# Weight fold from split parts and bias sums off TensorE in an attention and mixture-of-experts kernel

## The chip, the cores and the metric

The kernel runs on one core of one Trainium2 chip. The metric is the device time in microseconds. Its engines are TensorE (PE in the profile, PEld for its weight loads), VectorE (DVE), ScalarE (ACT), GpSimd (POOL), and the queues that issue transfers, SyncE's (SP) above all.

## What is computed

x has two batches of 1024 rows of 512, so 16 tiles of 128 rows. Cut to what matters:

```python
xn = layernorm(x)
q, k, v = split(xn @ w_qkv.T + b_qkv)
s = softmax(q @ k.T / sqrt(512)) @ v @ w_out.T + b_out
h = silu(xn @ expert_w[e] + expert_b[e])       # 8 experts, top 2 per row
m = sum(full_w[e] * h[e]) @ proj_w + proj_b
y = xn + m
g = silu(norm_w * y / sqrt(mean(y * y) + 1e-6))
out = x + s * g
```

All of it is fp32 in and out.

## The kernel before

Products run in fp32r on split operands: a value is written as a high part (a ScalarE copy to fp32r) and a low part (the value less the high part, on VectorE or GpSimd), and `product` makes three matmuls of them, high by high, high by low, low by high. The kernel folds weights first. The value weights times the output weights give `nw`, so that a tile of xn times `nw` is already the projected value (`values`, "v"). The query weights times the key weights give `mw` (`fold_keys`, four of them, in the order FOLDS = 2, 0, 1, 3, "mw").

The order on each engine is written out by hand, with semaphores. The first 71 us go so:

- **SyncE** loads, slice by slice (c = 0 to 3), a slice of the value weights (`raw_v`), one of the output weights (`raw_o`) and two tiles of batch 0 of x (`xb`), then the query and key weights. Then it stores each normalised tile.
- **TensorE** folds the value weights as 16 fp32 matmuls on the raw weights (line 1411; the trace shows two records for each), then makes the value bias with four more (`bias_of_values`), with turns 0 and 1 between and after them. `turn(g)` transposes a normalised tile into `tp` (line 1391). `values(0, t)` are 12 matmuls each (lines 1385 to 1387), with `turn(t + 1)` ahead of tile t. Then come `fold_keys`, `bias_products` (16 matmuls with 1 or 2 stationary columns), turns 8 and 9, the second key fold, `turn_biases`, turns 10 and 11, and the third and fourth key fold, then the logits.
- **VectorE** takes the statistics of the eight tiles of batch 0 (`row_stats`), turns them to mean and inverse deviation in 16 small steps (`first_stats`), normalises tiles 0 and 1, and makes the low parts: `fold_low`, `lo(g)` (x of tile g, "xt_l"), `v_lo` ("v_l"). The statistics of batch 1 lie behind `v_lo` of tiles 3 to 6.
- **ScalarE** makes the high parts (`fold_high`, `hi`, `v_hi`, `qk_high`) and normalises tiles 2 to 15 (line 754).
- **GpSimd** issues the load of x's second batch (line 601), makes the low parts of the query and key weights (`t_l`, `pt_l`, line 607), and then the 23 small steps of `batch_stats` for batch 1 (lines 396 to 406).

A transposed tile or a value product waits for a bank: `turn(g)` for `lo(g - 2)`, `values(0, t)` for `v_lo(t - 2)` and for `lo(t)`.

## Time and profile before

| | us |
|---|---|
| median of 3 runs | 533.2 (532.65 to 533.26) |
| the profiled execution | 533.14 |
| its span | 531.4 |
| TensorE busy | 514.9 |
| VectorE busy | 267.9 |
| ScalarE busy | 201.2 |
| GpSimd busy | 199.7 |

The page is one profiled execution. Line numbers are those of the kernel before. A timeline gives the start and length of each instruction, or of a row of like ones with their count, and in brackets how long the engine had been idle before it and what ended that. A matmul record is longer than the distance to the next, since they are pipelined.

### The profile page before, as it was taken

To read this page: it belongs to the slowest core of one execution; us is meant where nothing else is said; L and a number is where in the kernel's file an instruction comes from. 1 tells how busy PE (TensorE), PEld (TensorE's weight loads), DVE (VectorE), ACT (ScalarE), POOL (GpSimd) and SP (SyncE) were. 2 spreads that over 40 slices of the span, in tenths; PEclk is the share of its full clock that TensorE was granted. 3 is DMA by queue.
4 is the path that set the end of the run, shared out by engine and by line. 5 is a ranking of instruction groups with operands and counts; after the bars stand their busy time and mean duration, and the time that the engine had idled before them with its cause. 6 is when DMAs were issued, how large, how long until landed. Compare 5 with 4: busy or idle time off the path is not lost.

```text
span 531.4 us, 7656 instructions
## 1 busy us (share of the span) xinstructions
PE 514.9 (97%) x2454; PEld 414.7 (78%) x2455; DVE 267.9 (50%) x428; ACT 201.2 (38%) x300; POOL 199.7 (38%) x316
## 2 busy tenths in 40 slices
PE   4999999999999999899999999999999999999995
PEld 2488667887888888788888888888888888888884
DVE  2557232856138255664444444444574854567552
ACT  0265542222034254543333333323363552426550
POOL 3053210000007874243333330435457765266143
PEclk9999999999999799999999999999999999999999
DMA  8761277000100488857755554869523541242202
GB/s 265 270 239 39 93 243 299 0 21 20 41 0 1 178 278 297 283 192 228 245 172 165 165 161 145 301 237 307 169 79 100 198 146 52 83 152 65 79 37 83
DMA packets 37130, 81.40 MB, mean 153 GB/s; under 512 B 4128, under 2 KB 4144, under 8 KB 37104
## 3 DMA queue, kind: packets, MB, share of 16 engines
q1 hardware_dynamic: 27312, 50.60, 26.8%
q0 software_dynamic: 7920, 27.03, 16.6%
q10 hardware_dynamic: 1872, 3.41, 2.2%
q8 instruction: 17, 0.28, 0.2%
q14 instruction: 9, 0.07, 0.0%
HBM read 56.13 MB, written 24.90 MB: 152 GB/s over the span
## 4 chain that ended last, share of the span: by engine, by line
PE 91%; DVE 2%; DMA 2%; issue 1%; POOL 1%; ACT 1%; SPq 0%; ACTq 0%; DVEq 0%
PE ab L1385 19%; PE ab L1387 19%; PE ab L1386 19%; PE tp L1391 9%; PE sc L1385 6%; PE sc L1387 6%; PE sc L1386 6%; PE sc L1411 3%; DMA y_scratch<-yt 1%; DMA raw_o<-in_w_out_t 1%; PE tp L1562 1%; PE sc L1472 1%; PE ab L1419 1%; PE sc L1475 1%; DVE yt L1253 0%
## 5 line engine op out<-in xcount | busy, mean ns | idle before, releaser
L1385 PE MATMUL ab<-W,st_h 128*128 x156 | 64.5, 414 | 1.7 <-DVE st_l L1118 1.7
L1387 PE MATMUL ab<-W,st_l 128*128 x156 | 61.4, 394 | 0.0
L1386 PE MATMUL ab<-W,st_h 128*128 x156 | 60.9, 390 | 0.0
L863 ACT ACTIVATE yt<-yt 128x512 f32<-128x512 f32 x39 | 24.7, 632 | 75.9 <-DVE yt L1253 75.9
L1385 PE MATMUL sc<-xt_h,t_h 128*128 128x512 f32 x128 | 51.5, 403 | 0.0
L1387 PE MATMUL sc<-xt_h,t_l 128*128 128x512 f32 x128 | 50.9, 398 | 0.0
L1386 PE MATMUL sc<-xt_l,t_h 128*128 128x512 f32 x128 | 50.8, 397 | 0.0
L1118 DVE TENSOR_TENSOR st_l<-tp,st_h 128x512 fp32r<-128x512 f32 x40 | 27.7, 691 | 38.9 <-ACT st_h L859 29.2
L664 POOL DMA_INDIRECT y<-y_scratch,pos x32 | 31.0, 970 | 40.8 <-DMA y_scratch<-yt 20.6
L618 POOL TENSOR_TENSOR tile_hot<-in_tile,ids 128x640 fp32r<-128x640 f32 x2 | 6.5, 3242 | 90.0 <-DVE in_tile L1167 90.0
L1253 DVE TENSOR_TENSOR yt<-ab,bias_e 128x512 f32<-128x512 f32 x39 | 27.0, 692 | 26.2 <-PE ab L1387 22.1
L1385 PEld LDWEIGHTS ab<-W,st_h 128*128 128x128 f32 x156 | 29.4, 188 | 7.0 <-issue 2.2
L1184 DVE TENSOR_REDUCE small<-sc 128x1 f32<-128x1024 f32 x16 | 19.6, 1224 | 29.7 <-PE sc L1387 29.6
L1387 PEld LDWEIGHTS ab<-W,st_l 128*128 128x128 f32 x156 | 29.2, 187 | 6.7
L1386 PEld LDWEIGHTS ab<-W,st_h 128*128 128x128 f32 x156 | 29.5, 189 | 5.1
L1008 DVE SCALAR_TENSOR_TENSOR t_l<-ab,tb,t_h 128x512 fp32r<-128x512 f32 x16 | 12.0, 750 | 35.6 <-ACT t_h L773 35.0
L1387 PEld LDWEIGHTS sc<-xt_h,t_l 128*128 128x128 f32 x128 | 24.6, 192 | 5.3
L1386 PEld LDWEIGHTS sc<-xt_l,t_h 128*128 128x128 f32 x128 | 24.8, 193 | 5.0
L1385 PEld LDWEIGHTS sc<-xt_h,t_h 128*128 128x128 f32 x128 | 24.8, 193 | 5.0
L773 ACT ACTIVATE t_h<-ab,tb 128x512 fp32r<-128x512 f32 x16 | 11.0, 690 | 42.2 <-PE ab L1387 42.2
L637 POOL DMA_INDIRECT xn<-xn_scratch,idx x20 | 20.3, 1014 | 15.1 <-POOL idx L635 15.1
L635 POOL COPY idx<-token 128x1 int32 (+1 forms) x39 | 8.8, 226 | 45.5 <-PE tp L1391 45.5
(271 smaller groups left out, 1268.4 us busy)
## 6 DMA issues: line engine op xcount, KB each, us to landing
y_scratch<-yt SPq DMA_DIRECT2D x39, 256.0 KB
xb<-in_expert_w POOLq DMA_DIRECT2D x6, 1024.0 KB, 6.3
xn_scratch<-xs SPq DMA_DIRECT2D x16, 256.0 KB, 2.0
x<-in_x SPq DMA_DIRECT2D x16, 256.0 KB, 3.2
xb<-in_x SPq DMA_DIRECT2D x4, 512.0 KB, 8.6
xb<-in_x POOLq DMA_DIRECT2D x2, 1024.0 KB, 6.8
nw_scratch<-nw SPq DMA_DIRECT2D x1, 2048.0 KB, 13.1
mw_scratch<-mw SPq DMA_DIRECT2D x1, 2048.0 KB, 18.3
```

What stands on the lines that cost most here:

```text
L637: pool.indirect_dma_start(rows[q], None, xn_d, bass.IndirectOffsetOnAxis(idx[:, q:q + 1], 0)).then_inc(xg_in[q], 16)
L664: pool.indirect_dma_start(y[:, q, :], None, y_d, bass.IndirectOffsetOnAxis(pos[:, GB * s + p:GB * s + p + 1], 0))\
L863: nc.scalar.activation(yt[:, h, :], yt[:, h, :], ACT.Silu).then_inc(silu_d, 1)
L1008: vec.scalar_tensor_tensor(low[:, n, :], bank(("t", b, i, n)), tb[:, n:n + 1], high[:, n, :], ALU.add, ALU.subtract).then_inc(ab_read, 1)
L1118: vec.tensor_tensor(st_l[:, h, :, :], tp[:, h, :, :], st_h[:, h, :, :], ALU.subtract).then_inc(g_lo, 1)
L1184: link(vec.tensor_reduce(small[:, at, 0:1], sc[:, n % 2, :, :], AX.XY, ALU.max, negate=True))
L1253: vec.tensor_tensor(yt[:, h, :], ab[:, (U["e", 0] + h) % 2, :], bias_e[:, ds(e, 1), :].rearrange("p a n -> p (a n)"), ALU.add).then_inc(ab ...
L1385: nc.tensor.matmul(dst, lh, rh, start=start, stop=False)
L1386: nc.tensor.matmul(dst, lh, rl, start=False, stop=False)
L1387: return nc.tensor.matmul(dst, ll, rh, start=False, stop=stop)
L1391: last = nc.tensor.transpose(tp[:, h, c, :], src[:, c * P:(c + 1) * P], ident[:, :])
L1411: last = nc.tensor.matmul(sc[:, n // 2, n % 2, :], raw[2][:, c, n * P:(n + 1) * P], raw[3][:, c, :], start=(c == 0), stop=(c == KC - 1))
```

## The change

The value weights and output weights are split like everything else: high parts on ScalarE, the low part of a value slice on GpSimd (`vr_l`), that of an output slice on VectorE (`o_lo`), and the fold is made with `product`, 48 matmuls. Turns 0 and 1 stand before its last slice, and each later turn stands behind the values of two tiles earlier.

The biases no longer pass through TensorE as products. For the value bias, ScalarE scales each slice of the output weights by its bias column (`oa`), GpSimd adds the four, and TensorE sums over the rows with one product by ones. For the query and key bias, ScalarE scales the first slice and VectorE adds the others (`add_to_sum`, `acc`), TensorE transposes the sums (`sum_biases`) and VectorE reduces them (`fold_biases`), which now stands ahead of `lo(8)`.

The first two tiles of x are loaded first. VectorE's `first_stats` covers these two only; GpSimd's `batch_stats` does tiles 2 and 3, then 4 to 7, then batch 1. Its body is the old one, over the given columns.

```diff
+            def load_x(n):
+                w = slice(2 * n, 2 * n + 2)
+                sp.dma_start(xb[:, w, :], x_v[0][:, w, :]).then_inc(x_in[n], 16)
+            load_x(0)
             for c in range(KC):
                 sp.dma_start(raw[2][:, c, :], wqkv_v[2][:, c, :]).then_inc(vo_in[c], 16)
                 sp.dma_start(raw[3][:, c, :], wout_v[:, c, :]).then_inc(vo_in[c], 16)
-                w = slice(2 * c, 2 * c + 2)
-                sp.dma_start(xb[:, w, :], x_v[0][:, w, :]).then_inc(x_in[c], 16)
+            for n in range(1, KC):
+                load_x(n)
             for n in (0, 1):
                 sp.dma_start(raw[n][:, :, :], wqkv_v[n]).then_inc(qk_in[n], 16)
...
-            pool.wait_ge(vecs, 1)
+            for c in range(KC):
+                pool.wait_ge(vo_hi, 2 * c + 1)
+                pool.tensor_tensor(vr_l[:, c, :], raw[2][:, c, :], vr_h[:, c, :], ALU.subtract).then_inc(v_low, 1)
+            pool.wait_ge(v_low, KC)
+            pool.wait_ge(o_low, KC)
+            pool.wait_ge(oa_done, KC)
             for h in range(2):
                 w = slice(h * GB // 2, (h + 1) * GB // 2)
                 pool.dma_start(xb1[:, w, :], x_v[1][:, w, :]).then_inc(x1_in[h], 16)
+            pool.wait_ge(st_done, 1)
+            batch_stats(pool, link, slice(2, 4))
+            pool.wait_ge(st_done, 2)
+            batch_stats(pool, link, slice(4, GB))
+            pool.tensor_tensor(oa[:, 2, :], oa[:, 2, :], oa[:, 3, :], ALU.add).then_inc(oa_sum, 1)
+            pool.tensor_tensor(oa[:, 0, :], oa[:, 0, :], oa[:, 1, :], ALU.add).then_inc(oa_sum, 1)
+            pool.wait_ge(oa_sum, 2)
+            pool.tensor_tensor(oa[:, 0, :], oa[:, 0, :], oa[:, 2, :], ALU.add).then_inc(oa_sum, 1)
             for m in range(4):
                 high, low = ((wq_h, wq_l), (wk_h, wk_l))[m // 2]
@@ -606,8 +640,8 @@
                 pool.wait_ge(q_hi, m + 1)
                 pool.tensor_tensor(low[:, c, :], raw[m // 2][:, c, :], high[:, c, :], ALU.subtract).then_inc(qk_split, 1)
-            pool.wait_ge(st1_done, 1)
-            batch_stats(pool, link, 1)
+            pool.wait_ge(st_done, 3)
+            batch_stats(pool, link, slice(GB, G))
...
+            for c in range(KC):
+                act.wait_ge(vo_in[c], 32)
+                nc.scalar.copy(vr_h[:, c, :], raw[2][:, c, :]).then_inc(vo_hi, 1)
+                nc.scalar.copy(or_h[:, c, :], raw[3][:, c, :]).then_inc(vo_hi, 1)
+            act.wait_ge(vec_in, 32)
+            for c in range(KC):
+                nc.scalar.mul(oa[:, c, :], raw[3][:, c, :], bcols[:, 2, c:c + 1]).then_inc(oa_done, 1)
+            hi(0)
+            hi(1)
             for n in range(KC):
                 fold_high(n)
-            hi(0)
+            act.wait_ge(xn_ready, 2)
             act.wait_ge(ln_done, 1)
-            act.wait_ge(xn_ready, 2)
+            normalise(2)
+            normalise(3)
             for t in range(GB):
+                v_hi(0, t)
                 if t + 2 < GB:
-                    normalise(t + 2)
-                if t + 1 < GB:
-                    hi(t + 1)
+                    hi(t + 2)
+                if t == 0:
+                    for m in range(2):
+                        act.wait_ge(qk_in[1 - m], 16)
+                        nc.scalar.mul(acc[:, m, :], raw[1 - m][:, 0, :], bcols[:, m, 0:1]).then_inc(acc_0, 1)
+                if t == 1:
+                    act.wait_ge(ln_done, 2)
                 if 1 <= t < 5:
-                    qk_high(t - 1)
-                v_hi(0, t)
-            act.wait_ge(ln_done, 2)
+                    normalise(t + 3)
+                if 2 <= t < 6:
+                    qk_high(t - 2)
+            act.wait_ge(ln_done, 3)
             for g in range(GB, GB + 4):
                 normalise(g)
             fold_high(KC)
-            act.wait_ge(vecs, 2)
-            nc.scalar.copy(bias_rows, ab[0:2, :, :].rearrange("p a n -> p (a n)")).then_inc(rows_out, 1)
             hi(GB)
             hi(GB + 1)
...
-                dve.wait_ge(vecs, 1)
-                vec.tensor_tensor(sbias[:, :], ab[:, 1, :], bo_bc, ALU.add).then_inc(pre_done, 1)
+                vec.tensor_tensor(sbias[:, :], sc[:, 0, 1, :], bo_bc, ALU.add).then_inc(pre_done, 1)
...
-                dve.wait_ge(vecs, 3)
-                two = lambda m: ab[:, 0, 2 * KC * m:2 * KC * (m + 1)].rearrange("p (c a) -> p c a", a=2)
-                vec.tensor_reduce(tb[:, :], two(0), AX.X, ALU.add).then_inc(pre_done, 1)
-                link(vec.tensor_reduce(rw[:, :, E], two(1), AX.X, ALU.add))
-                vec.tensor_reduce(rb_bc[:, E:E + 1], ab[:, 0, 4 * KC:5 * KC], AX.X, ALU.add).then_inc(pre_done, 1)
+                dve.wait_ge(vecs, 1)
+                turned_sums = lambda m: ab[:, m, :].rearrange("p (c n) -> p c n", c=KC)
+                vec.tensor_reduce(tb[:, :], turned_sums(0), AX.X, ALU.add).then_inc(pre_done, 1)
+                link(vec.tensor_reduce(rw[:, :, E], turned_sums(1), AX.X, ALU.add))
+                fold_value_bias()
+                vec.tensor_reduce(rb_bc[:, E:E + 1], sc[:, 1, 1, 0:KC], AX.X, ALU.add).then_inc(pre_done, 1)
                 link(vec.tensor_copy(rw_hl[:, :, 0, :], rw[:, :, :]))
                 vec.tensor_tensor(rw_hl[:, :, 1, :], rw[:, :, :], rw_hl[:, :, 0, :], ALU.subtract).then_inc(pre_done, 1)
-                dve.wait_ge(pre_done, 4)
...
-            for t in range(GB):
+            def o_lo(c):
+                dve.wait_ge(vo_hi, 2 * c + 2)
+                vec.tensor_tensor(or_l[:, c, :], raw[3][:, c, :], or_h[:, c, :], ALU.subtract).then_inc(o_low, 1)
+            def add_to_sum(m, c):
+                if c == 1:
+                    dve.wait_ge(acc_0, m + 1)
+                last = vec.scalar_tensor_tensor(acc[:, m, :], raw[1 - m][:, c, :], bcols[:, m, c:c + 1], acc[:, m, :],
+                                                ALU.mult, ALU.add)
+                if c + 1 < KC:
...
+            dve.wait_ge(x_in[0], 16)
+            row_stats(0, 0)
+            link(row_stats(0, 1))
+            steps = first_stats(vec, link)
+            next(steps)
+            o_lo(0)
+            next(steps)
+            o_lo(1)
+            next(steps, None)
+            normalise(0)
+            normalise(1)
+            o_lo(2)
+            o_lo(3)
+            for t in range(2, GB):
                 if t % 2 == 0:
                     dve.wait_ge(x_in[t // 2], 16)
                 last = row_stats(0, t)
-            link(last)
-            first_stats(vec, link)
-            normalise(0)
-            fold_low(0)
...
+                if t in (3, GB - 1):
+                    last.then_inc(st_done, 1)
             lo(0)
-            for n in range(1, KC):
+            lo(1)
+            for n in range(KC):
                 fold_low(n)
-            fold_value_bias()
             for t in range(GB):
-                if t + 1 < GB:
-                    lo(t + 1)
                 v_lo(0, t)
+                if t + 2 < GB:
+                    lo(t + 2)
+                if t in (1, 2):
+                    for c in range(1, KC):
+                        add_to_sum(t - 1, c)
...
             fold_low(KC)
+            fold_biases()
             lo(GB)
             lo(GB + 1)
             fold_low(KC + 1)
-            fold_biases()
             lo(GB + 2)
             lo(GB + 3)
...
-            for c in range(KC):
-                pe.wait_ge(vo_in[c], 32)
-                for n in range(KC):
-                    last = nc.tensor.matmul(sc[:, n // 2, n % 2, :], raw[2][:, c, n * P:(n + 1) * P], raw[3][:, c, :],
-                                            start=(c == 0), stop=(c == KC - 1))
-                    if c == KC - 1:
-                        last.then_inc(fold, 1)
...
-            def bias_products():
...
-            def turn_biases():
...
+            def sum_biases():
+                pe.wait_ge(acc_d, 2)
+                for m in range(2):
+                    for n in range(KC):
+                        nc.tensor.transpose(ab[:, m, n * P:(n + 1) * P], acc[:, m, n * P:(n + 1) * P], ident[:, :])
+                pe.wait_ge(oa_sum, 3)
+                nc.tensor.matmul(sc[:, 0, 1, :], ones[:, :], oa[:, 0, :], start=True, stop=True)
+                pe.wait_ge(pre_done, 1)
+                nc.tensor.matmul(sc[:, 1, 1, 0:KC], ones[:, :], prod, start=True, stop=True).then_inc(vecs, 1)
...
             pe.wait_ge(const, 9)
-            bias_of_values(0)
-            bias_of_values(1)
-            turn(0)
-            bias_of_values(2)
-            bias_of_values(3).then_inc(vecs, 1)
+            for c in range(KC):
+                if c == KC - 1:
+                    turn(0)
+                    turn(1)
+                pe.wait_ge(v_low, c + 1)
+                pe.wait_ge(o_low, c + 1)
+                for n in range(KC):
+                    w = slice(n * P, (n + 1) * P)
+                    last = product(sc[:, n // 2, n % 2, :], vr_h[:, c, w], vr_l[:, c, w], or_h[:, c, :], or_l[:, c, :],
+                                   c == 0, c == KC - 1)
+                    if c == KC - 1:
+                        last.then_inc(fold, 1)
             for t in range(GB):
-                if t + 1 < GB:
-                    turn(t + 1)
                 pe.wait_ge(lo_done, t + 1)
-                if t == 1:
-                    pe.wait_ge(pre_done, 1)
                 values(0, t)
+                if t + 2 < GB:
+                    turn(t + 2)
             pe.wait_ge(qk_split, 4)
             fold_keys(FOLDS[0])
             pe.wait_ge(ab_read, 2 + GB)
-            bias_products()
+            sum_biases()
             turn(GB)
             turn(GB + 1)
             fold_keys(FOLDS[1])
-            turn_biases()
             turn(GB + 2)
             turn(GB + 3)
+            pe.wait_ge(pre_done, 5)
             fold_keys(FOLDS[2])
             fold_keys(FOLDS[3])
-            pe.wait_ge(pre_done, 4)
```

**The order on VectorE around values 1 to 4.** Names: `tp` and `ab` are in PSUM, `prob` holds the sums `acc`. Before:

```order
L990 TENSOR_TENSOR xt_l<-tp,xt_h 128x4x128
L1003 TENSOR_TENSOR v_l<-ab,v_h 128x512
L990 TENSOR_TENSOR xt_l<-tp,xt_h 128x4x128
L1003 TENSOR_TENSOR v_l<-ab,v_h 128x512
L990 TENSOR_TENSOR xt_l<-tp,xt_h 128x4x128
```

Now:

```order
L1047 TENSOR_TENSOR v_l<-ab,v_h 128x512
L1034 TENSOR_TENSOR xt_l<-tp,xt_h 128x4x128
L1176 SCALAR_TENSOR_TENSOR prob<-raw_k,bcols,prob 128x512 x3
L1047 TENSOR_TENSOR v_l<-ab,v_h 128x512
L1034 TENSOR_TENSOR xt_l<-tp,xt_h 128x4x128
L1176 SCALAR_TENSOR_TENSOR prob<-raw_q,bcols,prob 128x512 x3
L1047 TENSOR_TENSOR v_l<-ab,v_h 128x512
L1034 TENSOR_TENSOR xt_l<-tp,xt_h 128x4x128
```

Six scaled additions have come between the low parts of tiles 1 and 3 (values) and 3 and 5 (x).

**The order on GpSimd from the last constant load to the query and key weights' low parts.** Before:

```order
L594 DMA rb_bc<-in_router_b 128x8
L601 DMA xb<-in_x 128x4x512 x2
L607 TENSOR_TENSOR t_l<-raw_q,t_h 128x1024 x2
L607 TENSOR_TENSOR pt_l<-raw_k,pt_h 128x1024 x2
L396 TENSOR_TENSOR small<-stats 128x8
```

Now, with the two sets of 23 small steps that start at L406 cut out of the middle; first the head, then the tail:

```order
L612 DMA rb_bc<-in_router_b 128x8
L617 TENSOR_TENSOR vr_l<-raw_v,vr_h 128x512 x4
L625 DMA xb<-in_x 128x4x512 x2
L406 TENSOR_TENSOR small<-stats 128x2
L407 TENSOR_TENSOR small<-small 128x2
```

The tail, from the last small step of tiles 4 to 7 to the first of batch 1:

```order
L416 TENSOR_SCALAR shift<-small 128x4
L632 TENSOR_TENSOR oa<-oa 128x512
L633 TENSOR_TENSOR oa<-oa 128x512
L635 TENSOR_TENSOR oa<-oa 128x512
L641 TENSOR_TENSOR t_l<-raw_q,t_h 128x1024 x2
L641 TENSOR_TENSOR pt_l<-raw_k,pt_h 128x1024 x2
L406 TENSOR_TENSOR small<-stats 128x8
```

The query and key weights' low parts have moved behind two sets of statistics and three additions.

**The order on VectorE at the first key fold's low part.** Before:

```order
L1015 TENSOR_TENSOR mw<-sc,mw 128x512
L990 TENSOR_TENSOR bt_l<-tp,bt_h 128x4x128 x2
L1015 TENSOR_TENSOR mw<-sc,mw 128x512
L1028 TENSOR_REDUCE tb<-ab 128x4
L1029 TENSOR_REDUCE rw<-ab 128x4
```

Now:

```order
L1059 TENSOR_TENSOR mw<-sc,mw 128x512
L1071 TENSOR_REDUCE tb<-ab 128x4
L1072 TENSOR_REDUCE rw<-ab 128x4
L1063 TENSOR_TENSOR sbias<-sc,so 128x512
L1074 TENSOR_REDUCE rb_bc<-sc 128x1
L1075 CAST rw_hl<-rw 128x4x10
L1076 TENSOR_TENSOR rw_hl<-rw,rw_hl 128x4x10
L1034 TENSOR_TENSOR bt_l<-tp,bt_h 128x4x128 x2
```

The bias steps stand ahead of the low parts of tiles 8 and 9, and the two reductions each read 512 elements where they read 8.

## Rows read from the trace of the kernel before

**Rows 1.** The page, busy time of each engine, and its clock line.
```profile
PE 514.9 (97%) x2454; PEld 414.7 (78%) x2455; DVE 267.9 (50%) x428; ACT 201.2 (38%) x300; POOL 199.7 (38%) x316
...
PEclk9999999999999799999999999999999999999999
```

**Rows 2.** What TensorE waited for: total us, times, longest.
```profile
PE sc L1411 <- DMA raw_o<-in_w_out_t: 7.2, 1, 7.2
PE ab L1385 <- DVE st_l L1118: 1.7, 1, 1.7
...
PE tp L1391 <- ACT xs L754: 0.7, 1, 0.7
```

**Rows 3.** Timeline of TensorE: start us, us, engine line op [idle before <-releaser].
```profile
7.21 15.91 PE L1411 MATMUL sc<-raw_o,raw_v 128*128 128x512 f32 x32 [7.21 <-DMA raw_o<-in_w_out_t]
22.96 1.88 PE L1419 MATMUL ab<-raw_o,prob 128*128 128x512 f32 x4
...
27.19 0.47 PE L1385 MATMUL ab<-nw,xt_h 128*128 128x512 f32 x1
...
30.04 0.60 PE L1391 MATMUL tp<-ident,xs 128*128 128x128 f32 x4
...
59.52 1.36 PE L1391 MATMUL tp<-ident,xs 128*128 128x128 f32 x8 [0.68 <-ACT xs L754]
...
65.28 0.47 PE L1385 MATMUL sc<-pt_h,t_h 128*128 128x512 f32 x1
```

**Rows 4.** Timeline of VectorE: first statistics, first small step, a split beside GpSimd.
```profile
8.50 1.29 DVE L979 BATCH_NORM_STATS2 stats<-xb 128x6 f32<-128x512 f32 x2 [0.45 <-DMA xb<-in_x]
...
18.41 0.17 DVE L416 TENSOR_TENSOR small<-stats 128x8 f32<-128x8 f32 x1
...
34.07 0.69 DVE L1003 TENSOR_TENSOR v_l<-ab,v_h 128x512 fp32r<-128x512 f32 x1 [1.33 <-ACT v_h L769]
```

**Rows 5.** Timelines of ScalarE and of GpSimd, 33 to 60 us.
```profile
35.12 1.06 ACT L760 CAST t_h<-raw_q 128x1024 fp32r<-128x1024 f32 x1
...
58.65 2.93 ACT L754 ACTIVATE xs<-xb,shift,rstd 128x512 f32<-128x512 f32 x4 [5.61 <-POOL shift L406]
...
33.05 2.40 POOL L607 TENSOR_TENSOR t_l<-raw_q,t_h 128x1024 fp32r<-128x1024 f32 x1 [4.25 <-ACT t_h L760]
...
52.02 0.21 POOL L396 TENSOR_TENSOR small<-stats 128x8 f32<-128x8 f32 x1 [6.98 <-DVE stats L979]
...
58.38 0.23 POOL L406 TENSOR_SCALAR shift<-small 128x8 f32<-128x8 f32 x1
```

**Rows 6.** Timelines of VectorE and GpSimd where they overlap, and one VectorE line.
```profile
170.59 2.70 DVE L1186 TENSOR_TENSOR small<-small,logits 128x1 f32<-128x1 f32 x1
...
168.68 4.59 POOL L624 TENSOR_TENSOR W<-xb,W 128x2048 fp32r<-128x2048 f32 x1
...
419.88 3.30 DVE L1307 TENSOR_TENSOR yy<-yy,nrm_bc 128x512 f32<-128x512 f32 x1
...
420.08 1.30 POOL L670 TENSOR_TENSOR yy<-yy,pb_bc 128x512 f32<-128x512 f32 x1
421.33 1.29 POOL L674 TENSOR_TENSOR xb<-xb,pb_bc 128x512 f32<-128x512 f32 x1
...
480.47 3.40 DVE L1282 SCALAR_TENSOR_TENSOR y<-y,w 128x512 f32<-128x512 f32 x2
...
481.58 1.75 POOL L674 TENSOR_TENSOR xb<-xb,pb_bc 128x512 f32<-128x512 f32 x1
...
L1282 DVE SCALAR_TENSOR_TENSOR y<-y,w x16: 739/744/1774, 350.8 to 482.1; 128x512 f32<-128x512 f32 x16
```

**Rows 7.** TensorE's weight loads, and busy us by engine over a stretch.
```profile
10.79 0.34 PEld L1411 LDWEIGHTS sc<-raw_o,raw_v 128*128 128x128 f32 x1 [0.52 <-issue]
11.37 0.19 PEld L1411 LDWEIGHTS sc<-raw_o,raw_v 128*128 128x128 f32 x1 [0.25 <-issue]
...
178.00:182.00 4.00, 4.00 (x16) 3.52 (x16) 0.20 (x1) 2.28 (x2) 2.02 (x3) 0.54 0.47 144
```

65 lines of the change are left out of this document (28 added, 37 removed).

## The prediction

> **What bounds the kernel now.** I read the page first: TensorE is busy in 514.9 of 531.4 us [rows 1]. The list of what it waited for then names the gaps, all small: 7.2 us for the first weights, later 1.7 us once and, in this stretch, 0.7 us [rows 2]. So the span is TensorE's work plus a start, and the change touches only the first 71 us. There I read TensorE's timeline [rows 3]: the weight fold starts at 7.21, the first value product at 27.19, one tile of values takes 3.2 us with its transposes, the batch 1 tiles are turned from 59.52 after the 0.68 us wait, and the third key fold starts at 65.28. The other engines' timelines say what stands ready beside it: VectorE [rows 4], ScalarE and GpSimd [rows 5]. What the reader should see there [rows 5] is a chain that TensorE does not show: GpSimd's statistics of batch 1 run from 52.02 to 58.61, ScalarE normalises from 58.65, and TensorE's turn at 59.52 waits for that. It starts at VectorE's last statistics, one tile before the end of the values. Anything saved on TensorE between 52 and 59 us becomes waiting.
>
> **The fold's start.** Before, the first 512 KB of the load queue (a value and an output slice) are in at 7.21 and the next 512 KB (two x tiles) at 8.50 [rows 3, 4]. They change places, so I take x at 7.2 and the slices at 8.5. The new fold also needs all four parts. A ScalarE copy of 128x1024 takes 1.06 [rows 5], so two of 128x512 end near 9.1 and 9.6; GpSimd's subtraction is half of 2.40, so 1.2, and runs 9.2 to 10.4; VectorE's takes 0.7. If the two subtractions ran side by side the first product would start at 10.5. I do not think they do. At 170.59 a VectorE instruction on a single column with two SBUF inputs takes 2.70 us and ends just as GpSimd's subtraction of 168.68 (4.59 long) ends; at 480.47 two VectorE additions take 3.40 where the kind's median is 0.74, and GpSimd's addition beside them takes 1.75 instead of 1.30 [rows 6]. VectorE instructions that read PSUM show nothing of it: v_l takes 0.69 at 34.07 beside a GpSimd subtraction [rows 4, 5]. So two instructions of that sort queue for one another, each for the other's whole length. VectorE's subtraction then runs after GpSimd's, to 11.1, and the fold starts there; if GpSimd's second one gets in between, at 12.6. Bounds 10.5 and 13; I take 11.1.
>
> The fold was 16 fp32 matmuls, 7.21 to 22.96. It becomes 48 of the kind that follows each other in 0.23 ((30.04 - 27.19 - 0.1) / 12 [rows 3]), 11.0 us, plus 0.9 for turns 0 and 1 inside it. The first 4 us of any start ran at half pace: weight loads took 0.34 until 11.13 and 0.19 from 11.37 [rows 7], at 1.2 and then 2.4 GHz. That costs 2.0 us again. About 0.5 goes to the second slice, since three GpSimd subtractions in a row push VectorE's square-root steps (0.17 and a gap, so 0.2 each [rows 4]) and its second subtraction to 16.3. Sum: 11.1 + 11.0 + 0.9 + 2.0 + 0.5 = 25.5. Turn 1 and the four value-bias matmuls that stood before 27.19 are gone or inside this. Values start **1.7 us earlier**. Splits of the folded weights arrive 0.5 us ahead of each use: one costs nothing.
>
> **The values, tiles 0 to 4.** GpSimd issues x's second batch only after VectorE's fourth subtraction (19.5), 1.5 us, and then has two sets of statistics, each 23 small steps like those of 52.02 to 58.61, so 6.6 us; the narrower tiles do not help, since a step is 0.2 long and 0.09 apart. They end near 27.6 and 34.4. Normalising tile 4 waits for the second, and so does turn 4: 35.5 instead of 34.8. Gain left: **1.0 us**. Queued behind that wait on ScalarE are the splits of values 2, whose bank has a tile of slack.
>
> **The values, tiles 1 and 2: the sums.** This is the step that decides. VectorE gets six additions of 128x512 with two SBUF inputs, 0.74 each, three after lo(3) and three after lo(4). Alone they are 2.3 us per tile in 3.2 us of TensorE work, of which v_l and x_l need 1.3, so they would just fit. But GpSimd has its three additions of oa (1.3 each) from 34.7, and then the q/k subtractions, 2.4 us each, once ScalarE has made the high half, which comes some 3 us after a tile's values (tile 1's end near 33.3, the half at 36.2 [rows 3, 5]). All read SBUF. The first three sums alternate with oa's additions and end at 37.1 instead of 36.0. The second three start at 38.3; each waits behind a GpSimd instruction: 1.3, then 2.4, then 2.4. 38.3 + 3 x 0.74 + 6.1, less what overlaps, is near 46.1. Behind them on VectorE stand v_l(3) and x_l(5), 1.3 us, so tile 5 is ready at 47.5. TensorE is through with tile 4 and turn 6 at 42.4. It idles **5.1 us**, and the gain of 1.0 becomes a loss of 4.1. From both sides: no meeting at all gives 0; one 2.4 us meeting gives 2 us; all of GpSimd's halves before the last sum give 7.
>
> **Clock.** What lifts and drops TensorE's pace is seen so: after 7.2 us without work it starts at half, and over 178 to 182 the granted clock is 0.54, behind the 32 small matmuls of the slot table [rows 7]. That is the one low slice of the page's clock line [rows 1], so the 1.7 us gap near 220 cost no clock. A gap of 5.1 lies between 1.7 and 7.2, nearer to 7.2. I take one fall, at the price of the start's, **2.0 us**. The Trainium skill, "TensorE: Matmul & The Clock Gate" (Part 1), says that the phase against which idleness is judged is not tied to the kernel, so the same gap may or may not cost this; by that rule the sum would end 2.0 lower in some executions. The loss is now 6.1.
>
> **From the values to the third key fold.** Removed: 16 bias matmuls of 0.23 (3.7) and the turning of their rows (0.9); the added eight transposes (0.9), a fp32 product (0.86) and a small one take 2.1. The 2.5 us saved before turn 8 are nothing, because turn 8 waits on the statistics chain, which moves with the values: the wait of 0.7 becomes 2.7. Then the order changes. VectorE now does fold_biases before lo(8): two reductions of 512 elements (no row has one; v_l, as many elements from PSUM, takes 0.69 [rows 4]), sbias 0.6, and four small ones, 2.5 us together. Counted from ScalarE's normalise(8) at 58.65 in the old clock: four of them to 61.6, high fold 62.1, low fold 62.7, biases 65.2, lo(8) and lo(9) 66.5, turn 11, third key fold at 66.9. It was 65.28, so **1.6 us more**, after an idle of 2.6 us. Bounds 1.2 to 2.2.
>
> **Sum.** -1.7 + 0.7 + 5.1 + 2.0 + 1.6 = +7.7. The profiled execution took 533.14 with a span of 531.4, the median of the runs is 533.2. After the third fold the order is as before and TensorE is the bound, so the shift stays: 533.2 + 7.7 = 540.9, and I say **541.0 us**.
>
> **Rivals.**
> *The sums fit.* If VectorE's second set slips between GpSimd's halves or meets only part of one, the stall is at most 1 us and no clock falls: -1.0 + 1.6 + 0 to 1 gives 533.8 to 534.8. Against it: three sums and two halves share the same 5 us. 8 in 100.
> *The port plays no part.* The other side. Then the fold starts at 10.5, values come 2.8 us earlier, nothing later stalls, and 1.6 is given back: -1.2, **532.0 us**. It decides from the point where the gain at the start exceeds 1.6. Its condition is that the rows of [rows 6] are something else than a shared port; I see no other reading. 7 in 100.
> *It starts late and stalls long.* Start at 12.6, all three second sums behind GpSimd's halves (stall 7), and a second clock fall around turns 8 to 11, where TensorE does little for 3 us twice: 533.2 + 9.5 + 4 = 546.7. 8 in 100 above 545.5.
> *Not what it says.* If the three products ran slower than 0.23 each, as fp32, the fold would be over 20 us long and values 9 us later; the very form stands at 0.23 [rows 3]. 1 in 100, in the case above.
> The Trainium skill, "SBUF — State Buffer" (Who interferes with whom), gives the port to whichever instruction starts first, for its whole length; by that rule a sum waits for one GpSimd half, and the stall is the 5.1 us above. The additions at 480.47 [rows 6] follow it, but the product at 419.88 waits for two GpSimd additions that both start after it (3.30 long); if the sums fare like that, two queued halves cost one sum 4.8 us, and the stall is the 7 us of the upper bound.
>
> **How the numbers follow.** Main case 0.77 (535.8 to 545.5: at the low end a stall of 2 and no clock fall, -1.0 + 2 + 1.6; at the high end the stall of 7, the late start and the fall); the two good rivals 0.15; the high one 0.08. The range, 534.5 to 545.5, leaves out the second rival, half of the first and the high one, about two in ten. About 0.2% is what a measurement of this kernel tells from no change, 1.1 us. Of the first rival half lies within that, of the second half: faster 0.06, same 0.07, slower 0.87.
>
> **What would show it.** First product at 11.1 and values from 25.5; VectorE's L1176 rows well over 0.74 beside GpSimd's L641; a TensorE gap of 5 us near 42 to 47 that ends at x_l; loads of 0.34 behind it; a 2.7 us gap that ends at a normalise and one of 2.6 that ends at bt_l; nothing else after 75 us. If L1176 rows all read 0.74 the main step is wrong.

## The result and the profile after

The changed kernel takes 539.4 us (median of 4 runs, 536.0 to 542.0) against 532.9 us for the kernel before (4 runs, 532.1 to 533.3): ratio 1.012, 95% interval 1.006 to 1.018. It is **slower by 6.5 us**, where 541.0 was predicted. The profiled execution took 541.95 with a span of 540.2; a second profile of the same kernel has a span of 537.9. In two of the series below one execution took far longer than the rest (1818 us in e1, 800 us in the kernel before timed beside it), and the intervals are without it.

The page of the changed kernel, its busy line:

```profile
PE 508.9 (94%) x2448; PEld 417.4 (77%) x2449; DVE 283.1 (52%) x431; ACT 208.5 (39%) x313; POOL 217.6 (40%) x369
```

TensorE has 6 us less to do than in [rows 1], and the span is 8.8 longer: it waits. What it waited for (total, times, longest), against [rows 2]:

```profile
PE sc L1454 <- DVE or_l L1171: 12.2, 1, 12.2
PE ab L1454 <- DVE st_l L1162: 4.6, 3, 2.7
PE ab L1454 <- DVE xt_l L1034: 4.0, 2, 2.9
PE tp L1460 <- ACT xs L788: 2.8, 1, 2.8
...
PE tp L1460 <- DVE bt_l L1034: 0.9, 1, 0.9
```

Four of the five lie in the first 72 us. Its timeline there, against [rows 3] (columns as there), with the third key fold as the last row:

```profile
12.24 0.77 PE L1454 MATMUL sc<-or_h,vr_h 128*128 128x512 f32 x1 [12.24 <-DVE or_l L1171]
...
40.49 0.50 PE L1454 MATMUL ab<-nw,xt_h 128*128 128x512 f32 x1 [1.07 <-DVE xt_l L1034]
...
46.85 0.50 PE L1454 MATMUL ab<-nw,xt_h 128*128 128x512 f32 x1 [2.89 <-DVE xt_l L1034]
...
64.71 1.82 PE L1460 MATMUL tp<-ident,xs 128*128 128x128 f32 x8 [2.79 <-ACT xs L788]
...
71.16 1.22 PE L1460 MATMUL tp<-ident,xs 128*128 128x128 f32 x8 [0.95 <-DVE bt_l L1034]
```

```profile
72.14 0.48 PE L1454 MATMUL sc<-pt_h,t_h 128*128 128x512 f32 x1
```

The third key fold stood at 65.28 before; it is at 72.14 now, **6.9 us later**. Who is late at 40.49 and 46.85 stands in the chain of work, cut to 33.9 to 46.8 us (start, us, what). L1176 is the line of the six scaled additions:

```profile
33.90 0.60 DVE xt_l L1034
34.49 1.35 DVE prob L1176
...
35.87 1.67 DVE prob L1176
...
37.57 1.67 DVE prob L1176
39.24 0.60 DVE v_l L1047
39.84 0.60 DVE xt_l L1034
40.44 1.60 DVE prob L1176
...
42.06 2.77 DVE prob L1176
...
44.85 0.75 DVE prob L1176
45.60 0.60 DVE v_l L1047
46.20 0.61 DVE xt_l L1034
```

Only the last of the six takes what such an addition takes alone, 0.75 (the kind's median in [rows 6] is 0.744). GpSimd's timeline beside it:

```profile
33.99 1.29 POOL L632 TENSOR_TENSOR oa<-oa 128x512 f32<-128x512 f32 x1
35.25 1.74 POOL L633 TENSOR_TENSOR oa<-oa 128x512 f32<-128x512 f32 x1
37.06 1.63 POOL L635 TENSOR_TENSOR oa<-oa 128x512 f32<-128x512 f32 x1
38.65 2.82 POOL L641 TENSOR_TENSOR t_l<-raw_q,t_h 128x1024 fp32r<-128x1024 f32 x1
41.83 2.44 POOL L641 TENSOR_TENSOR t_l<-raw_q,t_h 128x1024 fp32r<-128x1024 f32 x1 [0.35 <-ACT t_h L794]
```

The addition at 42.06 starts 0.2 after GpSimd's subtraction of 41.83 and ends at 44.83, 0.56 after it: it does its work once that is over. GpSimd pays too, with 1.74, 1.63 and 2.82 where it takes 1.29 and 2.40 alone.

After the wait TensorE runs at half pace for a while. Its timeline from 47.66 on: matmuls start 0.23 apart, then 0.43.

```profile
47.66 0.39 PE L1454 MATMUL ab<-nw,xt_h 128*128 128x512 f32 x1
47.88 0.59 PE L1455 MATMUL ab<-nw,xt_h 128*128 128x512 f32 x1
48.27 0.63 PE L1456 MATMUL ab<-nw,xt_l 128*128 128x512 f32 x1
...
50.83 0.62 PE L1456 MATMUL ab<-nw,xt_l 128*128 128x512 f32 x1
```

### The profile page after: what moved, and what is told of

Same layout as the page of the kernel before. It is cut to its first block, busy times and chain, and to the rows that moved or that the text cites. A ratio compares the mean times of both kernels' runs of the same rounds, so it can differ in the third digit from the quotient of the medians.

```text
span 540.2 us, 7718 instructions
## 1 busy us (share of the span) xinstructions
PE 508.9 (94%) x2448; PEld 417.4 (77%) x2449; DVE 283.1 (52%) x431; ACT 208.5 (39%) x313; POOL 217.6 (40%) x369
## 3 DMA queue, kind: packets, MB, share of 16 engines
q1 hardware_dynamic: 27312, 50.60, 25.7%
## 4 chain that ended last, share of the span: by engine, by line
PE 78%; DVE 7%; DMA 7%; POOL 3%; issue 2%; ACT 2%; DVEq 0%; ACTq 0%; POOLq 0%
PE ab L1454 17%; PE ab L1456 17%; PE ab L1455 17%; PE tp L1460 7%; PE sc L1454 6%; PE sc L1455 6%; PE sc L1456 6%; DMA xb<-in_expert_w 3%; DVE prob L1176 2%; POOL W L658 2%; DMA s_scratch<-so 1%; DMA y_scratch<-yt 1%; DMA so<-in_b_out 1%; PE sc L1521 1%; DVE W L1167 1%
## 5 line engine op out<-in xcount | busy, mean ns | idle before, releaser
L1454 PE MATMUL ab<-W,st_h 128*128 x156 | 65.7, 421 | 4.6 <-DVE st_l L1162 4.6
L1455 PE MATMUL ab<-W,st_h 128*128 x156 | 61.7, 395 | 0.0
L1454 PE MATMUL sc<-xt_h,t_h 128*128 128x512 f32 x128 | 50.3, 393 | 0.0
L1454 PE MATMUL ab<-nw,xt_h 128*128 128x512 f32 x60 | 25.1, 419 | 4.0 <-DVE xt_l L1034 4.0
```

The costliest lines, as they stand in the source:

```text
L1454: nc.tensor.matmul(dst, lh, rh, start=start, stop=False)
L1455: nc.tensor.matmul(dst, lh, rl, start=False, stop=False)
```

## The experiments

Each kernel was timed beside the kernel before and profiled once. This table, worked out from TensorE's timelines, gives the landmarks in us. "Rest" is the span less the start of the third key fold, so it holds everything that the change does not touch.

| kernel | fold | values | turn 8 | third key fold | span | rest | median us | ratio to before, 95% |
|---|---|---|---|---|---|---|---|---|
| before | 7.21 | 27.19 | 59.52 | 65.28 | 531.4 | 466.1 | 532.9 | |
| changed | 12.24 | 26.45 | 64.71 | 72.14 | 540.2 | 468.1 | 539.4 | 1.006 to 1.018 |
| changed, again | 12.34 | 25.8 | 64.61 | 72.04 | 537.9 | 465.9 | 539.6 | 1.009 to 1.016 |
| e1, no sums | 12.24 | 26.3 | 58.55 | 65.98 | 532.6 | 466.6 | 533.1 | 0.998 to 1.002 |
| e2, sums in PSUM | 12.36 | 25.9 | 58.19 | 65.61 | 529.8 | 464.2 | 534.3 | 1.002 to 1.007 |
| e3, halves in pieces | 12.24 | 26.0 | 64.58 | 72.01 | 536.9 | 464.9 | 539.7 | 1.009 to 1.018 |
| e4, lo first | 12.33 | 25.7 | 64.44 | 71.27 | 535.4 | 464.1 | 538.6 | 1.006 to 1.016 |
| e5, value lows on VectorE | 11.01 | 25.1 | 63.35 | 70.78 | 537.6 | 466.8 | 537.9 | 1.007 to 1.012 |
| e6, lows wait | 12.38 | 26.9 | 60.57 | 68.00 | 531.9 | 463.9 | 534.5 | 1.002 to 1.005 |
| e8, e2 and chain moved | 12.24 | 25.6 | 55.62 | 60.67 | 526.1 | 465.4 | 528.5 | 0.989 to 0.996 |
| e10, e8 again | 12.31 | 26.1 | 55.79 | 60.84 | 527.1 | 466.3 | 529.8 | 0.995 to 0.999 |
| b1, before and chain moved | 7.23 | 28.1 | 59.56 | 64.95 | 531.4 | 466.4 | 529.8 | 0.994 to 0.998 |
| e9, e8 and e5 | 10.77 | 24.3 | 53.97 | 59.02 | 522.3 | 463.3 | 527.1 | 0.989 to 0.993 |

Two cautions go with it. The kernel before was timed anew beside each group of kernels, and took 532.9, 532.3, 532.7 and 531.9 us, so medians of different groups compare to about 1 us. And a profile is one execution, not the median one: e2's took 531.5 where its median is 534.3, e9's 524.0 for 527.1, and b1's 533.2 for 529.8.

### Is it the sums? (e1, e2)

e1 leaves the six additions out:

```
-                    for c in range(1, KC):
-                        add_to_sum(t - 1, c)
+                    dve.wait_ge(acc_0, t)
+                    dve.sem_inc(acc_d, 1)
```

> The changed kernel without VectorE's six scaled additions into the query's and the key's bias sums (of each sum only ScalarE's first product is left, so that the biases of queries and keys come out incomplete); nothing else is touched. Theory (the six additions, 4.83 and 5.24 us for three each instead of three times 0.74, keep VectorE from tile 4's and tile 5's transposed copies): TensorE's two waits of 1.07 and 2.89 us for them go, and so does the half pace from 47.5 to 51.3 us, about 2 us; the third key fold starts at 66 to 67 us instead of 72.14, and the time falls from 539.4 to 533 to 535. Rival (VectorE is late there because of its statistics and copies, not of the sums): each wait keeps over 1 us, the third key fold stays at 70 us or later, and the time at 537 to 540. In both the wait before turn 8 (2.79 us, for ScalarE's copy) and that at tile 9 (0.95 us) stay, since the sums are done before them.

Measured: 533.1 us, the third key fold at 65.98, and both waits for xt_l are gone, with the half pace behind them. That is the theory: 66 to 67 and 533 to 535 were expected. One wait that was to stay did not, that for bt_l: the clock fell within turn 8 in this execution, and TensorE's slow work filled it. **The six additions cost 6.2 us at the third key fold (72.14 - 65.98) and about as much in the medians (539.4 - 533.1).** Each taken against the kernel before that was timed beside it, it is 5.7 us (6.5 less 0.8). The rest of the change together costs 0.7 at that point against the kernel before.

e2 keeps the additions, with their running sum in PSUM:

```
-                        nc.scalar.mul(acc[:, m, :], raw[1 - m][:, 0, :], ...)
+                        act.wait_ge(fold_l, KC)
+                        nc.scalar.mul(sc[:, 0, m, :], raw[1 - m][:, 0, :], ...)
...
+                dst = acc[:, m, :] if c + 1 == KC else sc[:, 0, m, :]
-                last = vec.scalar_tensor_tensor(acc[:, m, :], raw[1 - m][:, c, :], bcols[:, m, c:c + 1], acc[:, m, :],
+                last = vec.scalar_tensor_tensor(dst, raw[1 - m][:, c, :], bcols[:, m, c:c + 1], sc[:, 0, m, :],
```

> The changed kernel with the same six additions, but each running sum kept in a bank of PSUM until its last addition, which writes to SBUF as before. So an addition reads one operand in SBUF instead of two. Theory (the additions are long because VectorE and GpSimd contend for SBUF, and an instruction of VectorE with one operand there is not held up): the two sets of three take about 2.3 to 2.7 us each instead of 4.83 and 5.24, TensorE's waits of 1.07 and 2.89 us fall to 0.5 us at most in sum, the half pace after them goes, the third key fold starts at 66.5 to 67.5 us, and the time is 533.5 to 535.5. Rival (the additions are just more work than VectorE has room for, or the contention is the same for one operand): they take 4 us or more per set, the waits stay over 2 us in sum, and the time stays at 538 to 540, while the kernel without the additions falls to 533 to 535.

The added wait keeps ScalarE's first product off a bank that the fold still uses; that product starts at 30.1 us, and at 30.3 in the changed kernel. VectorE's and then GpSimd's timeline of e2:

```profile
33.91 1.54 DVE L1178 SCALAR_TENSOR_TENSOR sc<-raw_k,bcols,sc 128x512 f32<-128x512 f32 x2
35.49 0.75 DVE L1178 SCALAR_TENSOR_TENSOR prob<-raw_k,bcols,sc 128x512 f32<-128x512 f32 x1
...
37.35 1.54 DVE L1178 SCALAR_TENSOR_TENSOR sc<-raw_q,bcols,sc 128x512 f32<-128x512 f32 x2
38.92 0.75 DVE L1178 SCALAR_TENSOR_TENSOR prob<-raw_q,bcols,sc 128x512 f32<-128x512 f32 x1
```

```profile
34.09 1.29 POOL L632 TENSOR_TENSOR oa<-oa 128x512 f32<-128x512 f32 x1
35.35 1.29 POOL L633 TENSOR_TENSOR oa<-oa 128x512 f32<-128x512 f32 x1
...
38.07 2.42 POOL L641 TENSOR_TENSOR t_l<-raw_q,t_h 128x1024 fp32r<-128x1024 f32 x1
```

The same six additions in the same place, beside the same work of GpSimd: 2.3 us a set instead of 4.8 and 5.2, and GpSimd's are back at 1.29 and 2.42. The edit changes where the running sum is read, in all six, and where it is written, in the first two of each set. The third of a set still writes to SBUF, beside a GpSimd instruction in both sets, and takes 0.75 as well; so it is the reading that counts, one operand in SBUF instead of two. The time is 534.3, as expected, and the third key fold at 65.61 stands 0.9 before the range. So it is not the amount of work, the rival's account, but the two operands. The Trainium skill, "SBUF — State Buffer" (Who interferes with whom), says that a VectorE instruction with at most one SBUF input (outside its two-port modes) does not contend with GpSimd, and that one with two does with a GpSimd instruction that reads SBUF; the rows agree, 0.75 against the 1.35 to 2.77 of the five additions that met GpSimd.

### Is it GpSimd? (e6, e3)

e6 leaves the additions as the change has them, and holds GpSimd's four low parts of queries and keys back until both sums are done:

```
                 pool.wait_ge(q_hi, m + 1)
+                if m == 0:
+                    pool.wait_ge(acc_d, 2)
```

> The changed kernel with GpSimd's four low parts of queries and keys held back until VectorE has made both sums, so that VectorE's second set of three additions meets no work of GpSimd, and the first still meets GpSimd's three additions of the output weights. Theory (the sums are long because GpSimd works on SBUF at the same time): the first set stays at 4 to 5 us, the second takes 2.3 to 2.7 us instead of 5.24, TensorE's wait of 2.89 us at tile 5 falls to under 0.5, that of about 1 us at tile 4 stays, the low parts run from about 43 to 53 us without holding the key fold up by more than 0.5, and the time is 535 to 537. Rival (VectorE is slow with two operands in SBUF whatever GpSimd does): both sets stay over 4 us, the wait at tile 5 stays near 2.9, and the low parts come later on top: 539 us or more.

VectorE's timeline of e6:

```profile
34.87 4.61 DVE L1178 SCALAR_TENSOR_TENSOR prob<-raw_k,bcols,prob 128x512 f32<-128x512 f32 x3
...
40.60 2.31 DVE L1178 SCALAR_TENSOR_TENSOR prob<-raw_q,bcols,prob 128x512 f32<-128x512 f32 x3
```

One kernel shows both: 4.61 for three additions beside GpSimd's additions of oa, 2.31 for the three that meet nothing. The wait at tile 5 is gone, that of 0.86 at tile 4 stays, and the time is 534.5: 0.5 us better than the lower end of what was expected.

e3 cuts GpSimd's four subtractions of 128x1024 into eight of 128x512:

```
-                pool.tensor_tensor(low[:, c, :], raw[m // 2][:, c, :], high[:, c, :], ALU.subtract)...
+                for k in range(c.start, c.stop):
+                    last = pool.tensor_tensor(low[:, k, :], raw[m // 2][:, k, :], high[:, k, :], ALU.subtract)
```

> The changed kernel with GpSimd's four low parts of queries and keys (two slices in one instruction, 2.4 to 2.8 us) in eight instructions of one slice each, about 1.2 us. Theory (an instruction of VectorE that comes while GpSimd's runs waits until that one is over): each addition of a sum waits 1.2 us at most instead of up to 2.4, but meets twice as many boundaries; the six additions take 8 to 9 us instead of 10.1, and TensorE's waits at tiles 4 and 5 2.5 to 3.5 us in sum instead of 4.0; third key fold at 70.5 to 71.8 us, time 538 to 539.5. Rival (what counts is that GpSimd is busy throughout, whatever the length of its instructions, as where VectorE waited through two of them in a row at 8.72 us): waits 3.9 to 4.3 us in sum, time 539 to 540.

Measured: waits of 1.36 and 2.85, 4.2 in sum, third key fold at 72.01, 539.7 us. **The rival was right in its numbers.** Pieces don't help: each addition waits for a shorter instruction, but there is one before every addition. The second set's three take 1.74, 1.68 and 1.64 where they took 1.60, 2.77 and 0.75, which is 5.06 against 5.12 in sum.

### The other edits (e4, e5)

e4 moves lo(8) and lo(9) ahead of fold_biases:

```
             fold_low(KC)
-            fold_biases()
             lo(GB)
             lo(GB + 1)
+            fold_biases()
```

> The changed kernel with VectorE's low parts of tiles 8 and 9 ahead of its bias sums (fold_biases, 67.89 to 70.29 us), as they would stand if the sums were made last. Theory (the bias sums ahead of the low parts delay them, as the sum of the prediction has it with 1.6 us): the wait of 0.95 us of turn 10 for bt_l goes, the third key fold starts about 1 us earlier (71.2 us), and the time falls by 0.7 to 1.2 us, to 538.2 to 538.8. Rival (the lower parts only move the wait to the next copy, or ScalarE's chain sets the third key fold): another wait of about the same length in its place, the time within 0.3 us of 539.4.

The third key fold is at 71.27, where the theory had 71.2 and the two profiles of the changed kernel have 72.14 and 72.04. The time, 538.6, can't be told from theirs (539.4 and 539.6). And the wait for bt_l did not simply go; another stands in its place, as the rival had it, since the third key fold itself needs the biases. TensorE's timeline of e4:

```profile
71.27 0.50 PE L1454 MATMUL sc<-pt_h,t_h 128*128 128x512 f32 x1 [1.60 <-DVE rw_hl L1076]
```

e5 gives the low parts of the value weights to VectorE:

```
-            for c in range(KC):
-                pool.wait_ge(vo_hi, 2 * c + 1)
-                pool.tensor_tensor(vr_l[:, c, :], raw[2][:, c, :], vr_h[:, c, :], ALU.subtract).then_inc(v_low, 1)
...
+                dve.wait_ge(vo_hi, 2 * c + 1)
+                vec.tensor_tensor(vr_l[:, c, :], raw[2][:, c, :], vr_h[:, c, :], ALU.subtract).then_inc(v_low, 1)
```

> The changed kernel with the low parts of the value weights made by VectorE (one 128x512 subtraction each ahead of that of the output weights), none by GpSimd. Theory (VectorE's small steps of 1.2 us at 8.7 to 14.7 are steps that wait for GpSimd's subtractions to end, and GpSimd's long stretch later decides the time anyway): those steps take 0.16 each, the first matmul of the fold starts at 10 to 11 us instead of 12.2 and the values at 25 to 25.8 instead of 26.4; but the six additions are as long as before, TensorE waits 0.5 to 1.2 us more for tiles 4 and 5, the third key fold is at 71.8 to 72.3, and the time 538.5 to 539.5. Rival (what comes earlier at the start stays): third key fold about 71.0, time 538.0 to 538.5.

Timelines of VectorE and GpSimd in the changed kernel:

```profile
8.72 1.18 DVE L428 SCALAR_TENSOR_TENSOR small<-small 128x2 f32<-128x2 f32 x1
9.93 1.24 DVE L429 SCALAR_TENSOR_TENSOR small<-small 128x2 f32<-128x2 f32 x1
```

```profile
8.61 2.54 POOL L617 TENSOR_TENSOR vr_l<-raw_v,vr_h 128x512 fp32r<-128x512 f32 x2 [3.01 <-ACT vr_h L812]
```

and VectorE's in e5:

```profile
8.97 0.16 DVE L428 SCALAR_TENSOR_TENSOR small<-small 128x2 f32<-128x2 f32 x1
9.16 0.16 DVE L429 SCALAR_TENSOR_TENSOR small<-small 128x2 f32<-128x2 f32 x1
```

Two steps on two columns each took 1.2 us, one GpSimd subtraction each. With the subtractions on VectorE they take 0.16, and the fold starts at 11.01, although VectorE has 2.4 us more to do. On the start the theory was right; on what follows the rival was: the waits at tiles 4 and 5 stayed at 0.99 and 2.92, and the 1.2 us carried through to the third key fold (70.78) and, as far as the intervals tell, the time (537.9, against 539.4 and 539.6). I had assumed that GpSimd's statistics pin the place of the stall. They don't: they stand behind its load of x's second batch, which waits for VectorE's last low part of the output weights, and that came earlier too (the load is issued from 18.11 in e5, from 19.64 in the changed kernel).

### A version that beats both (e8, e10, b1, e9)

In e2 two waits are left, 2.83 before turn 8 and 2.34 before turn 10:

```profile
58.19 1.36 PE L1462 MATMUL tp<-ident,xs 128*128 128x128 f32 x8 [2.83 <-ACT xs L788]
...
64.63 1.22 PE L1462 MATMUL tp<-ident,xs 128*128 128x128 f32 x8 [2.34 <-DVE bt_l L1035]
```

The first is the one that [rows 5] show as a chain: GpSimd's small steps, which in e2 run from 50.69 to 57.3, while VectorE has nothing to do. The second is for the bias steps ahead of lo(8), 61.36 to 63.8 in e2. e8 makes one edit for each: it puts the chain on VectorE in 17 steps, and fold_biases ahead of the first key fold's low part, where VectorE idles:

```
-            pool.wait_ge(st_done, 3)
-            batch_stats(pool, link, slice(GB, G))
...
             for t in range(GB):
+                if t == 7:
+                    dve.wait_ge(st_done, 3)
+                    w = slice(GB, G)
+                    steps = first_stats(vec, link, w)
+                    next(steps)
                 v_lo(0, t)
+                if t == 7:
+                    next(steps)
+                    next(steps, None)
+                    vec.scalar_tensor_tensor(shift[:, w], mean[:, w], -1.0, rstd[:, w], ALU.mult, ALU.mult)...
...
-            fold_low(KC)
             fold_biases()
+            fold_low(KC)
```

> The kernel with the running sums in PSUM, and in addition the second batch's chain of small steps for its means (GpSimd, 50.7 to 57.2 us there) on VectorE, in 17 steps, where VectorE has 8.6 us idle; its bias sums stand ahead of the low part of the second key fold. Theory (TensorE's wait of 2.8 us before tile 8's turn is for this chain, and the wait of 2.3 us before tile 10's for the bias sums behind the low part): VectorE's chain ends at 54 to 55 us, the first wait falls to 1 us at most and the second to 0.5, the third key fold starts at 62 to 63 us, and the time is 530 to 532, below the 534.3 of the kernel without the move and at or below that of the kernel before (532.3 in the same call). Rival (another chain is as late, such as ScalarE's four normalised tiles or the x loads): a wait of 2 us or more at tile 8 stays, time 533.5 to 534.5.

First and last of the steps on VectorE, and TensorE's turn of tile 8, in e8:

```profile
50.72 0.17 DVE L425 TENSOR_TENSOR small<-stats 128x8 f32<-128x8 f32 x1
...
54.55 0.17 DVE L1215 SCALAR_TENSOR_TENSOR shift<-mean,rstd 128x8 f32<-128x8 f32 x1
...
55.62 1.36 PE L1469 MATMUL tp<-ident,xs 128*128 128x128 f32 x8 [0.18 <-ACT xs L785]
```

A step is 0.20 from start to start on VectorE and 0.28 on GpSimd, and there are fewer. The third key fold is at 60.67, 4.9 us earlier than in e2, and the time 528.5, better than expected. No kernel has one edit without the other, but the landmarks part them: turn 8 comes 2.6 us earlier (58.19 to 55.62, its wait 2.83 to 0.18), which is the chain, and from there to the third key fold it is 5.05 instead of 7.42, **2.4 us that belong to the order of the biases**. The last three kernels:

> The kernel before, with nothing of the change but the second batch's chain of small steps moved from GpSimd (52.0 to 58.6 us) to VectorE in 17 steps, after the low part of the eighth tile's values (53.07 us). Theory (in the kernel before TensorE is busy up to 58.84 us, so that the chain holds up tile 8's turn by the 0.68 us of its wait and no more): the turn starts at 58.8 instead of 59.5, the third key fold at 64.6 instead of 65.3, and the time falls by 0.5 to 0.8 us, to about 532.0; the folded biases' gain can only be had with the change. Rival (the moved chain is worth in this kernel what it was worth on top of the change, 5 us): about 527.5 us.

> The kernel with the running sums in PSUM and the second batch's chain on VectorE once more, beside the two others of this call: 528 to 529 us, 0.5 to 1.1% below the kernel before, third key fold at 60.7 us.

> The same with the low parts of the value weights on VectorE too, so that the fold starts at 11.0 us instead of 12.2. Theory (with the sums and the chain out of the way, nothing takes back what the start gives): values from about 25.0, third key fold at 59.3 to 59.9 instead of 60.7, and 527.2 to 527.9 us where its twin takes 528.5. Rival (the next resource holds it: the normalised tiles 2 and 3 on ScalarE, whose scales GpSimd makes by 27.6 us, were 0.17 us late at tile 2's turn already): the turn of tile 2 waits 1 us or more, the third key fold stays at 60.5 or later, and the time within 0.5 us of the twin's.

b1 is the kernel before with the moved chain alone. It takes 529.8 (0.994 to 0.998), a gain of 0.9 to 3.1 us where 0.5 to 0.8 was expected: the 5 us of the rival are ruled out (and they were never the chain's alone), but the gain starts just above what the theory gave. Its one profile doesn't show that gain: it is of a slow execution (533.2). The start ran at half pace for 1.7 us longer, with weight loads of 0.34 until 12.85 where they ended at 11.13 in [rows 7]; so the fold ran 16.84 us instead of 15.91, the values start 0.9 later and the third key fold is at 64.95, not the 64.6 expected. The wait before turn 8 is gone, as expected. e10 repeats e8 at 529.8, 1.3 more than e8 and 0.8 above what was expected; the two intervals overlap. e9 adds e5's edit, has the values at 24.3 and the third key fold at 59.02, both a little earlier than its theory had them, and takes **527.1 us, 0.9% below the kernel before**; its interval lies below those of b1 and e10. So a fold in three products with biases summed on the vector engines can be had at a gain, once the sums read PSUM, the biases stand ahead of the key fold's low part, and the chain and the value weights' low parts are off GpSimd. Without the last of these the gain over b1 isn't shown: e10 and b1 have the same median, though e10's third key fold is 4.1 us earlier in the profiles. Of the 4.1, 0.9 is the slow start of b1's profiled execution; where the rest went isn't settled (next section).

## Why the prediction was right

**What bounds it, and that savings before turn 8 are lost.** Right: 2.79 us ending at a normalise, 2.7 predicted, and e8 shows the converse: with the chain on VectorE the wait is 0.18 and turn 8 comes 2.6 us earlier. The 2.7 doesn't follow from its terms, though. Of the 2.5 us called saved before turn 8, 0.9 (the turning of the bias rows) stands behind it, at 63.55 in the kernel before. That leaves 1.6, and 1.9 was measured (from the first key fold to the wait 4.74 us, 6.59 before); the chain came 0.3 later on top.

**The fold's start.** 12.24, the bound "12.6 if GpSimd's second one gets in between" and not 11.1. The case that was taken was wrong: GpSimd's second subtraction does get in. It doesn't meet VectorE's subtraction, which takes its plain 0.69 at 11.40, but the two small steps ahead of it, which the sum had left out; and the slices were in at 7.9, 0.6 earlier than assumed, so that it came out a little under the bound. Half pace followed. The 0.5 us for the second slice did not come: TensorE has no wait inside the fold. The values start at 26.45, in the second profile at 25.84, where 25.5 was predicted. So the gain is 0.7 to 1.4, not 1.7.

**Turn 4.** 35.61 against 35.5, and that is luck. TensorE doesn't wait there in either profile: the normalised tile is there at 34.88, and turn 4 stands directly behind values 2. It comes at 35.61 because the values began late, and at 35.10 in the second profile. The term of 0.7 us is zero.

**The sums.** Right in kind, and close in size:

| | predicted | changed | changed, again |
|---|---|---|---|
| first three end | 37.1 | 39.2 | 38.0 |
| second three end | 46.1 | 45.6 | 45.6 |
| TensorE waits (tiles 4, 5) | 5.1 | 1.07 + 2.89 | 0.40 + 4.12 |

The first set was mis-sized: the waits for oa's additions were put at 1.1 us in sum, and each addition met one in the first profile (1.35, 1.67, 1.67), two of three in the second (0.74, 1.67, 1.67). So tile 4 waits as well, which the prediction didn't have. The second was counted as if three waits of 1.3, 2.4 and 2.4 stood nearly in full, and has 0.85, 2.0 and none. The two errors partly cancel, which is luck: 4.0 and 4.5 us of waiting for 5.1. The upper bound of 7, one sum held by two queued halves, was not seen: in the second profile GpSimd's two halves run back to back (5.17 us from 39.17), and two additions wait for one each, 2.73 and 2.94 long. In these additions the rule that the prediction cites, one instruction for its whole length, fits all rows: each ends 0.55 to 0.57 after the GpSimd instruction that it waited for.

**Clock.** The predicted fall came. In the changed kernel the granted clock is 0.61 from 47 to 51 us, and 0.63 in the second profile. Priced at 2.0, it cost 1.6 in the first (eight matmuls 0.2 late each) and about 1.4 in the second (six to seven of them): the stretches at 1.2 GHz were shorter than at the start. A second fall, which the prediction had only in its rival of the long stall, came in the first profile within turn 8 (granted clock 0.50 from 65 to 68), and it was hidden: the wait for VectorE set turn 10.

**Turn 8 to the third key fold.** 7.43 us in both profiles against 5.76 before: 1.67 more, 1.6 predicted. But the wait at bt_l was called 2.6 and is 0.95 in the first profile, where the fall fills the rest, and 2.35 in the second, where the clock stays up. e4 bears out the cause by 0.8 to 0.9 us. The other 0.8 it moves to the third key fold itself, which now waits for the biases; only e8's order, which has them made while VectorE idles, takes both away.

**Sum.** At turn 8 the shift is 5.2 and 5.1 where the steps had 6.1; at the third key fold 6.9 and 6.8 where they had 7.7. Up to turn 8 the measured terms of the first profile are -0.7 + 0 + 4.0 + 1.6 = 4.9, those of the second -1.4 + 0 + 4.5 + 1.4 = 4.5; the last 0.3 to 0.6 is in none of them. In the medians the shift is 6.5, and 541.0 was 1.6 too high.

**The bounds and the chances.** The late start and the stall of 7 add 1.5 and 1.9 to the 7.7, which gives 544.3 for the top of the main case, where it says 545.5, and 546.3 for the high rival, where it says 546.7. By its own halves the chances would be 0.035 for faster, 0.075 for the same and 0.89 for slower.

**"Nothing else after 75 us."** The first profile has 2.0 us more of rest, and TensorE's wait for st_l is 4.6 us there instead of 1.7. This is not the change: the same kernel, profiled again, has 465.9 of rest, as before (466.1), and waits 2.4.

> The changed kernel as it is, profiled a second time. Theory (the loss of 6.9 us at the third key fold is the same in every execution, and what came on top of it after 75 us in the first profile, 1.9 us, is not): the third key fold starts at 72.1 us within 0.5, TensorE's two waits for xt_l are 4 us in sum, and the distance from the third key fold to the end of the span differs from the first profile's (468.1 us) by 1 to 3 us, with other waits for the expert stage's transposes (st_l, 4.6 us in the first). Rival (the change moves the later stages too): that distance is again within 0.3 us of 468.1, and 1.9 us longer than in the kernel before.

Over all kernels the rest lies between 463.3 and 468.1. TensorE's waits for these transposed copies from 200 to 232 us, in two profiles of each of two kernels (the changed one and its repeat, then e8 and its repeat e10):

```profile
PE ab L1454 <- DVE st_l L1162: 4.6, 3, 2.7
```

```profile
PE ab L1454 <- DVE st_l L1162: 2.4, 2, 2.1
```

```profile
PE ab L1463 <- DVE st_l L1160: 1.6, 2, 1.0
```

```profile
PE ab L1463 <- DVE st_l L1160: 4.2, 3, 2.0
```

Over all 13 profiles these waits sum to 0.5 (e6) to 4.6 us, 1.7 in the kernel before and 3.8 in b1, and the rest is mostly longer where they are longer. So this stage makes a part of the difference from one execution to the next; that it makes the spread of the changed kernel's runs (536.0 to 542.0) is likely, not shown. Whether an earlier arrival makes these waits longer on average, which would explain why e10's lead doesn't show against b1, was not tested.

## What to carry to other kernels

In every row here that was looked at, a VectorE instruction with two operands in SBUF that meets a running GpSimd instruction which reads SBUF waits until that one is over, even if it works on two columns; cost it with GpSimd's timeline beside it, not alone. Keeping a running sum in PSUM, or giving the work to one of the two engines only, took the wait away here; cutting GpSimd's work into halves didn't. And a saving on the engine that bounds the kernel counts only up to the next chain that it waits for: here 23 small steps of GpSimd hid 2.6 us that TensorE no longer needed, until they stood on an idle VectorE, and bias steps in an unlucky place hid another 2.4.
